# Attention stage: products with the values in two visits a head instead of three, with a place of its own for every block of probabilities

## The reference, cut to what matters

```
q = einsum('qdh,bcd->bhcq', Q, x) * sq      # same for k (K) and v (V)
att = einsum('bhcq,bhCq->bhcC', q, k) / d_query
att = where(causal, att, -inf)
p = softmax(att, axis=-1)
y = einsum('bhcC,bhCv->bhcv', p, v)
z = einsum('dvh,bhcv->bcd', W, y) * (...)
```

## Time and profile before

| what | value |
|---|---|
| median of 3 runs | 2114.48 us (2114.16 to 2121.46) |
| profiled execution, its own time | 2105.63 us |
| its span | 2103.9 us |
| TensorE clock, mean over the span | 0.941 of 2.4 GHz |
| PE busy | 1850.8 us, 88% of the span |
| DVE, ACT, POOL busy | 1361.6, 1077.4, 1178.6 us |

### The profile page before, as it was taken

The page is one execution under the profiler, slowest core; times in us unless marked ns, Lnnn a source line. Parts: engine busy times, 40 slices in busy tenths (PEclk is TensorE's granted clock), DMA queues, the critical chain, the costliest instruction groups (busy, mean ns, idle before and its releaser), DMA issues. The chain is left out here.

```text
span 2103.9 us, 39719 instructions
## 1 busy us (share of the span) xinstructions
PE 1850.8 (88%) x12071; PEld 1436.4 (68%) x12072; DVE 1361.6 (65%) x3652; ACT 1077.4 (51%) x2250; POOL 1178.6 (56%) x1159
## 2 busy tenths in 40 slices
PE   5863999999779999999999999999999999973870
PEld 2552888888657677777777777777787777753650
DVE  7884444444367887756878757887757887653763
ACT  5331333333356566656665646655646656522760
POOL 4355223332206566636687836687836687835782
PEclk9856999999989999999999999999999999977995
DMA  9853433333331221202121102111111121122979
GB/s 332 266 202 102 110 51 52 50 50 50 68 102 53 55 59 53 60 26 59 47 82 52 49 24 64 48 55 51 49 34 54 52 59 49 33 96 83 202 125 262
DMA packets 215683, 177.33 MB, mean 84 GB/s; under 512 B 85443, under 2 KB 200728, under 8 KB 214881
## 3 DMA queue, kind: packets, MB, share of 16 engines
q1 hardware_dynamic: 177904, 138.78, 22.6%
q0 software_dynamic: 28656, 27.61, 8.7%
q10 hardware_dynamic: 8960, 8.92, 1.2%
HBM read 95.05 MB, written 80.72 MB: 84 GB/s over the span
## 5 line engine op out<-in xcount | busy, mean ns | idle before, releaser
L953 POOL TENSOR_TENSOR c_den_late<-c_den_late,c_p 128x512 f32<-128x512 f32 (+3 forms) x384 | 410.1, 1068 | 129.7 <-ACT c_p L1268 84.1
L1268 ACT ACTIVATE c_p<-PS 128x512 f32<-128x512 f32 (+3 forms) x768 | 343.3, 491 | 208.6 <-PE PS L2487 100.4
L2499 PE MATMUL PS<-c_p,c_vh 128*64 128x256 f32 (+3 forms) x3072 | 292.5, 332 | 0.5 <-ACT c_yT L1250 0.5
L2479 PE MATMUL PS<-c_q,c_k 128*128 128x512 f32 (+2 forms) x768 | 283.3, 373 | 4.1 <-DMA c_q<-c_mr 2.5
L2456 PE MATMUL PS<-c_k,c_q 128*128 128x512 f32 (+2 forms) x768 | 268.5, 364 | 8.3 <-DVE c_max L1839 3.3
L889 POOL DMA_INDIRECT acc<-b_y,b_tok x71 | 110.5, 1557 | 272.2 <-ACT b_y L1138 245.3
L2480 PE MATMUL PS<-c_q,c_k 128*128 128x512 f32 (+2 forms) x768 | 258.2, 348 | 0.0
L2499 PEld LDWEIGHTS PS<-c_p,c_vh 128*64 128x64 f32 x3072 | 194.2, 136 | 87.7 <-issue 20.8
L1259 ACT ACTIVATE c_q<-PS 64x512 fp32r<-64x512 f32 x256 | 151.0, 590 | 158.9 <-PE PS L2443 155.6
L1839 DVE TENSOR_REDUCE c_max<-PS 128x1 f32<-128x512 f32 x256 | 175.4, 685 | 46.4 <-PE PS L2456 46.0
L953 POOL TENSOR_TENSOR c_den<-c_den,c_p 128x384 f32<-128x384 f32 (+2 forms) x192 | 141.3, 736 | 109.1 <-ACT c_p L1268 83.9
(11 more groups left out here) (304 smaller groups left out, 4031.5 us busy)
## 6 DMA issues: line engine op xcount, KB each, us to landing
c_vh<-c_v SPq DMA_DIRECT2D x64, 256.0 KB
c_rrow<-rden SPq DMA_DIRECT2D x63, 256.0 KB, 3.6
routed<-b_empty SPq DMA_DIRECT2D x32, 289.0 KB, 10.3
d_xe<-routed SPq DMA_DIRECT2D x32, 289.0 KB, 4.1
b_xt<-routed SPq DMA_DIRECT2D x71, 130.0 KB, 2.1
b_w12T<-in_w12T_dram SPq DMA_DIRECT2D x16, 512.0 KB, 13.9
d_acc<-acc SPq DMA_DIRECT2D x16, 512.0 KB, 9.1
c_st_hi<-wqk_split SPq DMA_DIRECT2D x48, 128.0 KB
```

Of the source, the lines that this page charges most:

```text
L953: pool.tensor_tensor(den[:, off:], den[:, off:], p, ALU.add).then_inc(s_cPa, 1)
L1268: act.activation(c_p[:, P_AT[h][m]:P_AT[h][m] + WIDTH[m]], PS[:, ST_BANK[m % STB], skip:skip + WIDTH[m]], ACT.Exp, scale=ATT_SCALE).then_i ...
L2479: pe.matmul(PS[:, bank, 0:n], c_k1[h][:, j * P:(j + 1) * P], c_q1[h][:, q], start=True, stop=False)
L2499: ins = pe.matmul(dst, c_vh[h][:, j, :], columns[:, :, a, :], start=(j == 0), stop=(t0 == 3))
```

## The change

- The visits are now two: blocks 0 to 3 where they were, and blocks 4 to 11 together, behind the chunks N0 to N3 and ahead of the next head's blocks 0 to 2.
- `c_p` has 4608 columns instead of 3328, and every block has its place. What ACT waits for before it writes a block follows from that. Room for it is made by laying `xn1` and `r_swb` over other buffers; `make_xn` gets one more wait.
- PE: blocks 9, 10, 11 follow right behind M11, with P3 between 10 and 11; then P4, P5, T, N0 to N3, the second visit, blocks 0 to 2 of the next head with their masks.
- ACT: `take_y` of query half 0 goes behind block 7 and the third high part; `take_max` goes behind block 11.
- DVE: the second `split_lo` goes ahead of M11; `normalise_y` goes behind N3.

```diff
-        ROUND = 4
-        ROUNDS = len(BLOCKS) // ROUND
+        FIRST_VISIT = 4
...
-        P_SIZE = R_SIZE[0] + R_SIZE[1]
-        R_AT = ((0, R_SIZE[0], 0), (R_SIZE[1], 0, R_SIZE[1]))
-        P_AT = [[R_AT[h][m // ROUND] + sum(WIDTH[m // ROUND * ROUND:m]) for m in range(len(BLOCKS))] for h in range(2)]
+        P_SIZE = sum(WIDTH)
+        P_AT = [sum(WIDTH[:m]) for m in range(len(BLOCKS))]
...
-                act.wait_ge(s_cPu, H * len(BLOCKS) + (m // ROUND * ROUND + ROUND))
-                act.wait_ge(s_cPa, H * len(BLOCKS) + (m // ROUND * ROUND + ROUND))
+                act.wait_ge(s_cPu, H * len(BLOCKS) + (FIRST_VISIT if m < FIRST_VISIT else len(BLOCKS)))
+                act.wait_ge(s_cPa, H * len(BLOCKS) + (m + 2 if m == FIRST_VISIT else m + 1))
...
                 probabilities(H, h, 6)
-                take_y(H, pair, h, 0, c_yT[hp % 2])
                 probabilities(H, h, 7)
                 if not fetch:
                     splits_hi(0, 2)
+                take_y(H, pair, h, 0, c_yT[hp % 2])
                 probabilities(H, h, 8)
...
-                if follows:
-                    take_max(H + 1, table)
                 probabilities(H, h, 9)
...
                 for m in (10, 11):
                     probabilities(H, h, m)
+                if follows:
+                    take_max(H + 1, table)
                 splits_hi(1, 0, 1, 2)
...
-                    maxima(10, 11)
+                    maxima(10)
                     if more:
                         split_lo(H + 2, h, 0, 1)
+                    maxima(11)
                 routing(2)
-                maxima_ahead(0, 1)
+                maxima_ahead(0, 1, 2, 3)
                 if h == 0 and zs:
                     normalise_y(pair - 1, c_yT[1 - hp % 2])
                 routing(3)
-                maxima_ahead(2, 3)
...
-                outputs_of(1)
+                for m in (9, 10):
+                    scores_t(H, h, m)
+                mask_t(9, 10)
+                if not fetch:
+                    projections(3)
+                scores_t(H, h, 11)
+                mask_t(11)
+                if not fetch:
+                    projections(4, 5)
                 if follows:
                     transpose_max(H + 1, table)
-                for m in (9, 10, 11):
-                    scores_t(H, h, m)
-                mask_t(9, 10, 11)
...
-                projections(3, 4)
-                maxima_ahead(0)
-                projections(5)
-                maxima_ahead(1)
-                maxima_ahead(2)
+                    projections(3, 4, 5)
+                maxima_ahead(0, 1, 2, 3)
+                outputs_of(1)
                 if follows:
-                    scores_t(H + 1, 1 - h, 0)
-                maxima_ahead(3)
-                if follows:
-                    for m in (1, 2):
+                    for m in (0, 1, 2):
                         scores_t(H + 1, 1 - h, m)
                     mask_t(0, 1, 2)
-                outputs_of(2)
```

More of the change, by code:

```diff
@@ L230, in network @@
         CHUNKS = [(t, c) for t in range(QT) for c in range(t // 4 + 1)]
-        ROUND = 4
-        ROUNDS = len(BLOCKS) // ROUND
+        FIRST_VISIT = 4
         WIDTH = [512 - max(0, j * P - c * 512) for c, j in BLOCKS]
-        R_SIZE = [sum(WIDTH[r * ROUND:(r + 1) * ROUND]) for r in range(ROUNDS)]
-        P_SIZE = R_SIZE[0] + R_SIZE[1]
-        R_AT = ((0, R_SIZE[0], 0), (R_SIZE[1], 0, R_SIZE[1]))
-        P_AT = [[R_AT[h][m // ROUND] + sum(WIDTH[m // ROUND * ROUND:m]) for m in range(len(BLOCKS))] for h in range(2)]
+        P_SIZE = sum(WIDTH)
+        P_AT = [sum(WIDTH[:m]) for m in range(len(BLOCKS))]
         ST_BANK = (4, 5, 1)
@@ L264, in network @@
         c_yT = [place(f"c_yT_{n}", [P, S]) for n in range(2)]
-        xn = [None, place("xn1", [P, G, D])]
-        c_spread = nc.alloc_sbuf_tensor_at("c_spread", [P, 4, NC2, DQ], F32, offset=at[0] - 4 * G * D)
+        c_spread = place("c_spread", [P, 4, NC2, DQ])
         after_heads = at[0]
-        R_BYTES = 27200
+        R_BYTES = 24576
         at[0] = top_at = (arena_end - 4 * 2 * KD * NH * DQ) // 32 * 32
@@ L275, in network @@
         assert after_heads <= r_at
-        r_swb = place("r_swb", [P, KD * E1 + KD * 2 * I1 + D], BF16)
         r_gwT = place("r_gwT", [P, KD, E1])
@@ L289, in network @@
         r_idx = place("r_idx", [P, G * K1, 1])
+        r_swb = nc.alloc_sbuf_tensor_at("r_swb", [P, KD * E1 + KD * 2 * I1 + D], BF16, offset=at[0])
         r_oh = place("r_oh", [P, G, K1, E1])
@@ L932, in head_adds @@
                     den = c_den[c][h]
-                    done, p = H * len(BLOCKS) + (m + 2 * ROUND), c_p[:, P_AT[h][m]:P_AT[h][m] + WIDTH[m]]
+                    done, p = H * len(BLOCKS) + (m + len(BLOCKS)), c_p[:, P_AT[m]:P_AT[m] + WIDTH[m]]
                     if c > 0 and j == 0:
@@ L947, in head_adds @@
                         pool.sem_inc(s_pass, 1)
-                        pool.tensor_tensor(den[:, :], c_p[:, P_AT[h][m - 1]:P_AT[h][m - 1] + WIDTH[m - 1]], p, ALU.add).then_inc(s_cPa, 2)
+                        pool.tensor_tensor(den[:, :], c_p[:, P_AT[m - 1]:P_AT[m - 1] + WIDTH[m - 1]], p, ALU.add).then_inc(s_cPa, 2)
                     else:
@@ L1189, in make_xn @@
                     act.sem_inc(s_pass, 1)
+                if g == 1 and not (isinstance(batch, int) and batch <= 1):
+                    act.wait_ge(s_scat[0], (batch - 1) * (16 * G * K1) + SCAT0)
+                    act.sem_inc(s_pass, 1)
                 for q in range(G):
@@ L1264, in probabilities @@
                 act.wait_ge(s_cT, H * len(BLOCKS) + (m + 1))
-                act.wait_ge(s_cPu, H * len(BLOCKS) + (m // ROUND * ROUND + ROUND))
-                act.wait_ge(s_cPa, H * len(BLOCKS) + (m // ROUND * ROUND + ROUND))
-                act.activation(c_p[:, P_AT[h][m]:P_AT[h][m] + WIDTH[m]], PS[:, ST_BANK[m % STB], skip:skip + WIDTH[m]], ACT.Exp,
+                act.wait_ge(s_cPu, H * len(BLOCKS) + (FIRST_VISIT if m < FIRST_VISIT else len(BLOCKS)))
+                act.wait_ge(s_cPa, H * len(BLOCKS) + (m + 2 if m == FIRST_VISIT else m + 1))
+                act.activation(c_p[:, P_AT[m]:P_AT[m] + WIDTH[m]], PS[:, ST_BANK[m % STB], skip:skip + WIDTH[m]], ACT.Exp,
                                scale=ATT_SCALE).then_inc(s_cP, 1)
@@ L2394, in _ @@
             finish_stage(pe, 1)
-            pe.sem_inc(s_cPu, 2 * ROUND)
-            pe.sem_inc(s_cPa, 2 * ROUND)
+            pe.sem_inc(s_cPu, len(BLOCKS))
+            pe.sem_inc(s_cPa, len(BLOCKS))
             pe.sem_inc(s_cP, STB)
@@ L2495, in outputs @@
                 pe.wait_ge(s_cP, H * len(BLOCKS) + (m + 1 + STB))
-                columns = c_p[:, P_AT[h][m]:P_AT[h][m] + WIDTH[m]].rearrange("p (t a q) -> p t a q", a=2, q=DQ)
+                columns = c_p[:, P_AT[m]:P_AT[m] + WIDTH[m]].rearrange("p (t a q) -> p t a q", a=2, q=DQ)
                 for a in range(2):
@@ L2582, in outputs_of @@
                 def outputs_of(r):
-                    for m in range(r * ROUND, (r + 1) * ROUND):
+                    for m in range(FIRST_VISIT) if r == 0 else range(FIRST_VISIT, len(BLOCKS)):
                         c, j = BLOCKS[m]
```

7 lines of the change are left out of this document (4 added, 3 removed).

## The result

| what | before | after |
|---|---|---|
| median of the runs | 2116.65 us (2114.16 to 2121.46, 4 runs) | 2225.48 us (2222.83 to 2227.01, 4 runs) |
| profiled execution, span | 2103.9 us | 2221.1 us |
| TensorE clock, mean over the span | 0.941 | 0.939 |

The change makes the kernel slower: ratio 1.0509, interval 1.0490 to 1.0527, which is 109 us. The two spans differ by 117.2, but some 12 of these are not the change.

The account below looks back on a forecast made before the run. PE bounds the kernel. Waits 1 and 2 less the visit gain (70.8), wait 3 (17.3), `rows_of` heads (6.6) and fetch heads (5.4) make +100 on 2105.6; 8.9 more for the median gives 2215 us, range 2165 to 2235.

Parts of the forecast that it names:

- A visit: On PE, removing one with both edges saves at most 0.37 us; 0.12 us a head counted as gain.
- Wait 1: PE at P3 waits for DVE's second low part, since visit two no longer stands ahead; 0.77 us a head lost.
- The floor of 0.6: Block 11 needs block 8's PSUM bank, freed by ACT, so 0.6 us stays lost even with a quicker DVE.
- Wait 2: N2 and N3 behind T wait for ACT's copy of T and DVE's maximum of N0; 0.55 us a head.
- Wait 3: Block 3 behind the masks waits for ACT to free block 0's bank; 0.79 us in each of 20 heads, three half.
- Sums by head: An even head grows by about 1.2 us, one followed at once by block 3 by about 2.0.
- more than counted: Rival: PE's waits pull others along, another 0.4 us in 59 heads, 24 us, 2227 to 2250; chance 0.10.
- Fetch heads: In three heads P3 needs three ACT copies and a low part, no longer covered by visit two; 1.8 us each, 5.4.
- Routing on DVE between M11 and N0: DVE's routing steps there could add up to 0.5 us in 24 heads, 12 us more, as an upper bound.
- The drain is all: Rival: P3, N2 and N3 find banks free; 62 heads save 0.12 to 0.37 us, 2092 to 2107; chance 0.05.
- Only part of the waits: Rival: one of waits 1 and 2 vanishes, 32 to 45 us less, 2165 to 2187; chance 0.14.
- The clock falls: Rival: a less busy PE drops to 1.2 GHz in stretches; some 50 us of them give above 2260; chance 0.02.

Follow-up runs that it names:

- four_visits: Kernel before's order in the changed kernel's buffers, with visit two cut in half by block 9, so four visits a head; 2137.20 us, 1.0083 of before.
- visit_back: Changed kernel with blocks 4 to 7 multiplied between M11 and block 9 again and `take_y` in its old place; 2184.95 us, 1.0307 of before.
- low_early_y_late: Changed kernel with the second `split_lo` ahead of M10's maximum on DVE and `take_y` behind block 8 on ACT; 2224.66 us, 1.0495 of before.
- t_early: Changed kernel with T moved ahead of P4 and P5; 2229.49 us, 1.0514 of before.
- t_early_spread: Changed kernel with T ahead of P4 and N0 between P4 and P5; 2211.51 us, 1.0439 of before.
- masks_apart: Changed kernel with each mask right behind its block 0, 1, 2 in odd heads and head 0 of a batch; 2213.16 us, 1.0442 of before.

## Why the prediction was right, step by step

The time fell 10 us above the predicted 2215 and inside the range. The mechanism, three waits in front of PE that the visits had covered, is what the runs show; that the sum came so near is in part luck, as told under its terms.

- **PE bounds the kernel, and only work on PE or a wait in front of it counts**: right. DVE's and ACT's busy times are as before (1363.5 and 1077.0 us).
- **A visit**: priced at most at 0.37 us; `four_visits` measured 0.34 to 0.36. `visit_back` takes back wait 1 and pays a visit, and 0.77 - 0.36 = 0.41 is what heads 12 and 13 show (0.43 and 0.40). Of the price, 0.12 was counted as won. The head that grew by 1.08 leaves more: with wait 1 at 0.78 and wait 2 at 0.57 it is 0.27, so 0.12 was too careful. No run measured this share by itself.
- **Wait 1**: 0.77 us, P3 at +3.72. Measured +3.74, by two small errors against each other: the low part ended 0.11 later than placed (895.33, +3.68), and the hand-over took 0.06, not 0.15. `visit_back` showed that the visit is what had covered it. The floor of 0.6 under it, from block 8's bank, was not tried. `low_early_y_late` doesn't test it: there ACT is done with block 8 earlier as well, and P3 (888.31) waits for a low part that DVE can't start before ACT's third high part (887.53).
- **Wait 2**: 0.55 us, the second visit at T + 1.42. Measured 1.43. That it has two limits was shown by `t_early` and `t_early_spread`.
- **Wait 3**: 0.79 us, block 3 at 0.95 behind the masks. Measured 0.91, since ACT starts 0.26 behind them and PE 0.05 behind ACT's end (885.34 to 885.39), not 0.08. Of the 17.3 us counted for it, 12.3 came back with `masks_apart`, where the masks in three groups cost something of their own.
- **Sums by head**: 1.2 and 2.0 forecast, 1.08 and 2.43 measured in batch 0. In batch 1 the same interval as head 12 went from 15.60 to 17.67, so 2.07. The extra in batch 0 is mostly P0's wait for the split weights, which the forecast missed: P0 stands 0.52 us behind the product ahead of it (887.14 to 887.66), before 0.23 (849.57 to 849.80); the rival "more than counted" named P0 of the next head as late, but for ACT's copies, and it was DVE.
- **Fetch heads**: 1.8 us each were counted. From block 6 to block 6 they grew by 2.35, 0.93 and 2.36; in batch 1 the kernel before had lost 1.5 us of its own in that head (23.06 against 21.54). Together 5.6 where the sum had 5.4. N3's wait (0.35 idle) was left out of it.
- **Routing on DVE between M11 and N0**: a bound of up to 0.5 us a head stood in the range, not in the sum. Measured: 2.40 in "slots" instead of 1.2, and so in three heads, 3.5 us more than counted.
- **Heads 2 to 4 of batch 0**: counted like the others, 4.4 us together. They grew by 2.75, 4.08 and 1.25 from block 6 to block 6, 3.7 more. The earlier trace rows had shown that DVE, not PE, sets the pace there, and the sum made nothing of it. Some 3 of the 3.7 are the two falls of the clock.
- **The sum**: from the first T to the last the kernel grew by 105.4 us where it said 100. The last two terms account for 7 us more than counted, and the remaining heads took 2 to 3 less. Errors of both signs are in it.
- **The waits of the profile were to grow by 80 to 100 us, busy time to stay**: wrong as a reading. PE's busy time grew by 38.9 us with the same instructions; from the first T to the last it was busy 38.5 us more and idle 66.8 more. The loss of a wait is the distance between starts; the tail of the matmul ahead covers part of it and is counted as busy. P3 starts 0.88 us behind two masks that need some 0.10, and shows as 0.59 idle. So the waits listed above add up to 74.4 us of the 105.
- **The rivals**: "The drain is all" is out (`visit_back`). "Only part of the waits" is out, all three are there. "The clock falls" is out as the cause, at some 3 of 109 us, but it happened: the granted clock fell to 1.2 GHz for 3.4 us behind the P3 waits of heads 2 and 3 of batch 0, and was 1.00 in the rest of the stage, with PE busy 95% of 850 to 1090 us. The Trainium skill ("TensorE: Matmul & The Clock Gate", A second HAM failure mode: psum-queue depth-cycling) tells of a kernel whose clock swung with short pauses between groups. Behind pauses of 0.6 us and less, several in every head, this trace shows no fall; it fell behind the two of 2.6 us. "More than counted" was right in kind, with two small things of it, and stayed below its 24 us.

Left open: why the clock falls behind one wait and not behind another of the same length (heads 2 and 4, both 2.64 us), and whether the 0.6 us floor under wait 1 is there.

## What to carry to other kernels

A piece of PE work is worth its own cost minus what it covers. Here the fixed part of a visit is 0.35 us, and the 1.2 to 1.9 us of products in it covered three hand-overs worth 0.6 to 0.8 us each. So before products are merged, list for each one what the engines behind PE do in its time, in the busiest head and not in the plain one: the two later attempts to keep the covers and win the 0.35 us came out even or ahead in some plain heads (15.93 and 15.25 against 15.89) and lost up to 4.8 us in single heads with routing, statistics or output products. Where two waits are moved in one kernel, expect them to meet. And where a wait got longer, look at the granted clock behind it before the loss is put down to the wait: one fall of it cost 1.3 to 1.7 us. Compare intervals only between points that have the same work between them in both kernels.

## What the runs showed of the hardware

- What a wait costs PE and what the profile calls idle ahead of it differ: 0.78 against 0.59 us at P3. Four waits of that kind a head are how PE's busy time could grow by 38.9 us with the same 12071 matmuls.
- The hand-over from ACT to the product that waits for it took 0.05 us at block 3 (885.34 to 885.39).
- The hand-over from a DVE `split_lo` to the product that waits for it took 0.06 us in a plain head (895.33 to 895.39) and 0.15 in a fetch head (938.47 to 938.62).
- With PE idle for 5% of 850 to 1090 us, in many waits of 0.6 us or less and one of 1.64, the granted clock stayed 1.00.
- Behind longer waits it fell to 1.2 GHz, for 3.4 us each time, in some cases and not in others. In the changed kernel: behind 2.64 and 2.60 us, not behind another 2.64, nor behind 1.64 in the fetch heads. In the kernel before: not behind three waits of 1.8 us. In `low_early_y_late`: behind 1.35 us at 1534.63, not behind 1.35 at 1877.01.
- Such a fall cost 1.3 us (head 4 of batch 0: `t_early` against the changed kernel) to 1.7 us (`low_early_y_late`, "slots").
